# Rebuilding the joint stage of a fused two-layer block: plain fp32 products, scatter in 32-row pieces, new engine order

## The reference, cut to what matters

```
x = x + tanh(g_xattn[0]) * L0_xattn(layernorm(x), ctx, ctx, Wq..bo)   # 16 heads, strided mask
x = x + tanh(g_ffn[0])   * L0_ffn(layernorm(x), controller, f1, f2, bias)
x = x + tanh(g_xattn[1]) * L1_xattn(layernorm(x), ctx, ctx, mask)
x = x + tanh(g_ffn[1])   * L1_ffn(layernorm(x), ln_g, ln_b, w1, w2)

L0_ffn:  grouped = 16 tokens a group; logits = grouped @ controller; perm = (logits == max over the group)
         sel = perm^T @ grouped; inner = relu(sel @ f1 + bias); inter = inner @ f2      # 64 slots a group
         out[token] = sum over slots of perm[token, slot] * inter[group, slot]           # the scatter
L1_xattn: softmax(x @ ctx^T * 512**-0.5 + mask * -1e9) @ ctx                             # one head of width 512
L1_ffn:  h = layernorm(x) * ln_g + ln_b; int8 of h by a quantile of |h|; ternary w1; gelu; int8; ternary w2
```

## Time and profile before

| | |
|---|---|
| Median of 3 runs | 1605.69 us (1605.4 to 1609.05) |
| The profiled execution | 1610.68 us, of which the span of the trace is 1608.6 us |
| Joint stage in the trace | 821.9 to 1138.2 us |
| PE / PEld / DVE / ACT / POOL busy over the span | 81% / 58% / 64% / 47% / 27% |

### The profile page before, as it was taken

How to read it: one execution, slowest core, us unless ns; L and a number is a source line. 1 busy time by engine, 2 the same in 40 slices (tenths; PEclk the granted TensorE clock), 3 DMA queues, 4 the chain that set the end, 5 groups by cost and what they waited for, 6 DMA issues and landing times. The chain is left out here.

```text
span 1608.6 us, 25261 instructions
## 1 busy us (share of the span) xinstructions
PE 1304.2 (81%) x9084; PEld 935.0 (58%) x9106; DVE 1027.0 (64%) x2374; ACT 759.1 (47%) x1145; POOL 433.5 (27%) x435
## 2 busy tenths in 40 slices
PE   6999999999999559999958999995142799244996
PEld 5788888888888347666425666664132444142442
DVE  5677667767776434444325787877396488776774
ACT  3233343434333214564323555553473555486991
POOL 1233333333333201110014878775100000000021
PEclk9999999999999769999979999997555799655998
DMA  6122231223121196885699888841300277322974
GB/s 219 45 71 73 87 105 66 73 85 105 66 73 62 49 338 223 295 314 223 249 289 275 241 229 241 229 145 40 109 1 3 111 307 305 142 79 69 419 298 157
DMA packets 100471, 261.81 MB, mean 163 GB/s; under 512 B 11120, under 2 KB 22544, under 8 KB 93200
## 3 DMA queue, kind: packets, MB, share of 16 engines
q1 hardware_dynamic: 88704, 226.82, 40.6%
q0 software_dynamic: 8688, 32.51, 6.2%
q10 hardware_dynamic: 2976, 1.14, 0.3%
HBM read 155.32 MB, written 105.12 MB: 162 GB/s over the span
## 5 line engine op out<-in xcount | busy, mean ns | idle before, releaser
L1203 PE MATMUL p_s<-p_rows,p_permT 128*128 128x512 f32 x256 | 132.2, 614 | 6.1 <-DMA p_rows<-inter_d 4.0
L922 PEld LDWEIGHTS p_sel<-p_pick,p_xp 128*128 128x128 bf16 x1536 | 91.4, 101 | 57.2 <-issue 32.6
L922 PE MATMUL p_sel<-p_pick,p_xp 128*128 128x128 bf16 x1536 | 102.5, 226 | 23.8 <-DVE p_pick L1044 12.5
L2267 POOL DMA_DIRECT2D p_y<-residual x8 | 10.8, 1347 | 404.8 <-POOLq L113 343.2
L1934 PE MATMUL p_z<-qT,w1T 128*128 128x512 bf16 x501 | 112.6, 385 | 3.0 <-PEq L113 2.5
L1060 DVE COPY p_selT<-p_sel 128x512 f32<-128x512 f32 x64 | 44.3, 692 | 104.6 <-PE p_sel L922 104.6
L2291 PE MATMUL p_o<-w2T,p_Gq 128*128 128x512 bf16 x376 | 85.2, 384 | 8.8 <-DVE p_Gq L2348 8.5
L1993 DVE MAX8 cand<-hid 128x8 f32<-128x128 f32 x384 | 74.7, 277 | 25.2 <-ACT hid L1981 25.2
L1934 PEld LDWEIGHTS p_z<-qT,w1T 128*128 128x128 bf16 x512 | 50.6, 99 | 64.7 <-issue 5.9
L1005 ACT ACTIVATE p_selT<-p_sel 128x512 f32<-128x512 f32 x64 | 38.2, 597 | 91.4 <-PE p_sel L922 91.4
L342 PE MATMUL p_M<-p_ctxTh,p_Wkh 128*128 128x256 f32 x256 | 76.0, 297 | 1.9 <-DVE p_Wkl L668 1.9
(11 more groups left out here) (335 smaller groups left out, 3910.2 us busy)
## 6 DMA issues: line engine op xcount, KB each, us to landing
inter_d<-p_stage SPq DMA_DIRECT2D x64, 512.0 KB, 4.0
p_rows<-inter_d SPq DMA_DIRECT2D x128, 256.0 KB, 5.3
activations<-hid SPq DMA_DIRECT2D x24, 1024.0 KB, 3.9
p_cin<-in_ctx_dram SPq DMA_DIRECT2D x32, 512.0 KB, 5.3
xparts<-p_parts SPq DMA_DIRECT2D x16, 768.0 KB, 3.2
hid<-activations SPq DMA_DIRECT2D x10, 1024.0 KB, 9.6
p_xp<-xparts SPq DMA_DIRECT2D x3, 3072.0 KB, 25.3
p_xin<-in_x_dram SPq DMA_DIRECT2D x16, 512.0 KB, 4.3
```

The lines of the kernel that those rows point to most:

```text
L922: mm = pe.matmul(bsel[u % 2][:, k * P:(k + 1) * P], xp[:, c, tile, r, :], pick[sb % 2][:, tile, :, :].rearrange("p s g -> p (s g)"), start ...
L1203: mm = pe.matmul(bo[t][:, :], permT[b % 2][:, t, k, :], R[b % 2][:, t, k, :], start=(k == 0), stop=(k == NK - 1))
```

## The change

It touches the joint stage, the DRAM layout of the two residuals, and the loads of the residual in the last stage. The scatter becomes four matmuls a tile, each writing 32 rows (two groups) of the output from 128 rows of `inter_d` (2 groups by 64 slots), with weights of 32 columns; the rows of a tile come in one DMA with partition g*64+s. `spread` and `permT` shrink to 2 groups, so a batch needs 2 turns. Scores and attention are single fp32 matmuls on unsplit data: no `turned_lows`, `e_low`, `values_high`, `values_low`; the values are `cin` itself. x is only centred before it is turned (`nm`), and the factor rstd*512**-0.5 (`rs`) is applied in `logits`. Keys are taken in the order (p t), so that a partition's part of ctx is one piece of 4 KB; the mask is permuted to match. Depths grow (XD 6, CD 5, two buffers of e, mx, z, rz), turned exponentials get the bank `bE`, which the turned perm shares, and STEPS is 21.

```diff
-    XD, CD = 4, 3
+    XD, CD, AHEAD = 6, 5, 2
-        spread = [sbt(f"spread{i}", [P, NT, SL, GR], BF16) for i in range(2)]
-        permT = [sbt(f"permT{i}", [P, NT, NK, P]) for i in range(2)]
+        spread = [sbt(f"spread{i}", [P, NT, GH, SL], BF16) for i in range(2)]    # GH = 2
+        permT = [sbt(f"permT{i}", [P, NT, P]) for i in range(2)]
-        rows = inter_d.rearrange("(n g) (k s) d -> n k s g d", g=GR, s=SK)
+        ct = ctx.rearrange("b (p t) d -> b p t d", t=NT)
+        rows = inter_d.rearrange("(n h g) s d -> n (g s) h d", h=GR // GH, g=GH)
-        STEPS = B + 4
+        STEPS = B + 5
@@ SP
             def load_rows(b, t):
-                for k in range(NK):
-                    sp.dma_start(R[b % 2][:, t, k, :], rows[b * NT + t, k])...
+                if b >= 2:
+                    sp.wait_ge(s[f"scattered{t}"], b - 1)
+                sp.dma_start(R[b % 2][:, t, :, :], rows[b * NT + t])...
             for i in range(STEPS):
+                if live(i + 1):
+                    load_rows(i + 1, 1)
+                    load_x(i + 1)          # waits hh_done of i-5, x_out of i-5
+                    load_ctx(i + 1)        # waits O_full of i-4
+                if live(i + 2):
+                    load_rows(i + 2, 0)
+                if live(i + 1):
+                    load_mask(i + 1)
+                if live(i - 4):
+                    store(i - 4)
@@ PE
+            def scatter(b, t):
+                pe.wait_ge(s["permT_done"], b + 1)
+                pe.wait_ge(s[f"r_in{b % 2}{t}"], 16 * (b // 2 + 1))
+                if b >= 1:
+                    pe.wait_ge(s[f"added{t}"], b)
+                for h in range(GR // GH):
+                    toks = slice(h * TH, (h + 1) * TH)                          # TH = 32
+                    mm = pe.matmul(bo[t][toks, :], permT[b % 2][:, t, toks], R[b % 2][:, t, h, :], start=True, stop=True)
             def scores(b, t):
-                terms = [(c, a, w) for c in range(C) for a, w in ((0, 0), (0, 1), (1, 0))]
+                for c in range(C):
+                    mm = pe.matmul(bS[:, t * S:(t + 1) * S], xnT[:, c, t * P:(t + 1) * P], ctxT[b % 2][:, c, :], ...)
             def attend(b, t):
-                terms = [(k, a, w) for k in range(NT) for a, w in ((0, 0), (0, 1), (1, 0))]
+                for k in range(NT):
+                    mm = pe.matmul(bO[t][:, :], eT[:, k, t, :], cin[b % CD][:, k, :], ...)
+            for i in range(STEPS):
+                attend(i - 3, 0); turn_ctx(i - 1, 0); turn_perm(i); turn_ctx(i - 1, 1); attend(i - 3, 1)
+                turn_xn(i - 1, 0); scatter(i, 0); turn_xn(i - 1, 1); scores(i - 1, 0); scatter(i, 1)
+                turn_e(i - 2); scores(i - 1, 1)
@@ ACT, each step
+                hidden(i - 4, 0); hidden(i - 4, 1); ctx_out(i - 1, 0); ctx_out(i - 1, 1); centred(i - 1, 0)
+                permT_out(i); centred(i - 1, 1); xn_out(i - 1, 0); xn_out(i - 1, 1); exps(i - 2)
+                magnitudes(i - 4); e_turned(i - 2)
@@ POOL, each step
+                rstd1(i - 2); spreads(i + 2); gains(i - 4); rstd2(i - 3)
@@ DVE, each step
+                maxima(i - 5); variance1(i - 1); logits(i - 2); attended(i - 3, 0); softmax(i - 2)
+                attended(i - 3, 1); scale_mask(i - 1); add(i, 0); variance2(i - 3); inverse(i - 2); add(i, 1)
+            def logits(b):
+                for t in range(NT):
+                    dve.scalar_tensor_tensor(e[b % 2][:, t, :], bS[:, t * S:(t + 1) * S], rs[b % 2][:, t:t + 1],
+                                             mks[b % 2]..., ALU.mult, ALU.add).then_inc(s["S_taken"], 1)
@@ rstd1 on POOL takes 3 small operations as before, rstd2 takes 4 in place of 9
@@ ffn
-                    pool.dma_start(y[i % 2][:, :, :], xv[:, order[i] * WB:(order[i] + 1) * WB, :])...
+                    pool.dma_start(y[i % 2][:, :, :], x3_d[:, order[i] * WB:(order[i] + 1) * WB, :])...
@@ mk_flamingo_gated
-    x_one, x_three = [dram(f"residual{i}", (B, S, D)) for i in range(2)]
+    x_one, x_three = dram("residual0", (B, P, NT, D)), dram("residual1", (P, TILES, D))
```

More of the change, by code:

```diff
@@ L1115, in phase2b3 @@
         bo, bT, bO = [[ps(f"{n}{i}") for i in range(2)] for n in "sTO"]
[L1116 to L1119, removed]
+        bS, bE = ps("S"), ps("E")
+        halves = "scattered added norm cT_full c_out nT_full n_out S_full O_full x3_done hh_done".split()
+        names = """const_in ident_in ln_in identb_done mask2_done tanh_done spread_done turned permT_done mean1 rstd1 mask_done S_taken soft exp
+            e_full e_out rz_done var2 rstd2 hg_done hid_done abs_done max_done own own_pool""".split() + \
+            [f"{n}{t}" for n in halves for t in range(NT)] + \
             [f"x_in{i}" for i in range(XD)] + [f"x_out{i}" for i in range(XD)] + [f"c_in{i}" for i in range(CD)] + \
@@ L1193, in _ @@
         @block.tensor
         def _(pe):
[L1196 to L1205, removed]
@@ L1220, in turn_tile, with turn_ctx @@
                 mm.then_inc(full, 1)
-            def turn_ctx(b):
+            def turn_ctx(b, t):
                 pe.wait_ge(s[f"c_in{b % CD}"], 16 * (b // CD + 1))
[L1224 to L1233, removed]
@@ L1235, in scores @@
-            def scores(b, t):
[L1236 to L1240, removed]
-                terms = [(c, a, w) for c in range(C) for a, w in ((0, 0), (0, 1), (1, 0))]
[L1242 to L1245, removed]
+                if b >= 1:
+                    pe.wait_ge(s[f"n_out{t}"], b)
@@ new lines, in _ @@
+                if live(i - 3):
+                    attend(i - 3, 0)
+                if live(i - 1):
+                    turn_ctx(i - 1, 0)
+                if live(i):
+                    turn_perm(i)
+                if live(i - 1):
+                    turn_ctx(i - 1, 1)
+                if live(i - 3):
+                    attend(i - 3, 1)
+                if live(i - 1):
+                    turn_xn(i - 1, 0)
+                if live(i):
+                    scatter(i, 0)
+                if live(i - 1):
+                    turn_xn(i - 1, 1)
+                    scores(i - 1, 0)
@@ L1289, in _ @@
+                if live(i):
+                    scatter(i, 1)
+                if live(i - 2):
+                    turn_e(i - 2)
+                if live(i - 1):
+                    scores(i - 1, 1)
         @block.scalar
@@ L1315, in hidden @@
-            def hidden(b):
+                    wait_all(act, "O_full", b)
+                act.activation(eT[:, :, :, :], bE[:, :].rearrange("p (k t q) -> p k t q", k=NT, t=NT), ACT.Copy).then_inc(s["e_out"], 1)
+            def hidden(b, t):
                 act.wait_ge(s["rstd2"], b + 1)
@@ L1378, in _, with after @@
             of_all = lambda a: a[:, :].rearrange("p (a d) -> p a d", a=1).broadcast_to([P, NT, D])
-            def small(out, a, c, op, sem=None):
-                pool.tensor_tensor(out[:, :], a, c, op).then_inc(sem or own, 1)
-                if sem is None:
-                    pool.wait_ge(own, n.next(own))
+            def after(op):
+                op.then_inc(own, 1)
+                pool.wait_ge(own, n.next(own))
             def spreads(b):
@@ L1418, in values_low @@
[L1418 to L1420 removed]
+                if b >= 2:
+                    wait_all(pool, "hh_done", b - 1)
+                after(pool.tensor_scalar(w5[:, :], mv2[b % 2][:, :, 1], 1.0 + EPS, EPS * EPS, ALU.mult, ALU.add))
+                after(pool.tensor_tensor(w6[b % 2][:, :], w5[:, :], mhalf[:, :], ALU.pow))
@@ L1492, in maxima, with softmax @@
+            def softmax(b):
+                dve.wait_ge(s["S_taken"], NT * (b + 1))
+                dve.tensor_reduce(mx[b % 2][:, :], e[b % 2][:, :, :], AX.X, ALU.max).then_inc(own, 1)
+                dve.wait_ge(own, n.next(own))
+                dve.tensor_scalar(mx[b % 2][:, :], mx[b % 2][:, :], -1.0, None, ALU.mult).then_inc(s["soft"], 1)
             def maxima(b):
```

380 lines of the change are left out of this document (160 added, 220 removed).

## The result

The changed kernel takes 1514.58 us in the median (1511.18 to 1516.68, 4 runs), the kernel before 1607.37 (1605.4 to 1609.73, 4 runs): ratio 0.9413 with an interval of 0.9399 to 0.9427. The prediction was 1514.0. The profiled execution took 1514.46, its span is 1512.7.

A forecast was written before the change was run, and what follows sets the result against it. PE was taken to bound the joint stage. Fill to 863, 12 steps of 12.0 us to 1007 and a 38.5 us drain end it at 1045.5; 91.3 and 0.4 us less bring the median from 1605.7 to 1514.0, range 1502 to 1549.

The forecast's parts named there:

- PE's sum: Joint stage, steady step: PE's scatter, mode switches, scores, attention and turns add up to 11.5 us.
- Handshakes: Joint stage, steady step: handshakes among PE at 11.5, DMA at 10.8 and DVE at 10.7 make the step 12.0 us.
- second rival: Joint stage: handshakes make each step 12.9 us, 80 us less in all, time 1525; chance 0.15.
- Fill: Start of the joint stage: DMA brings 12.8 MB at 355 GB/s, batch 3's last scatter ends at about 863.
- Drain: End of the joint stage: from the last scatter of batch 15 to the stage's end, 38.5 us.
- Rows: Joint stage DMA: the new row order gives 345 to 360 GB/s, 10.6 to 11.0 us a batch.
- 4 KB pieces: Larger pieces for x_mid and ctx: part of the faster joint-stage DMA; outside the stage, for x_mid, no gain.
- DVE: Joint stage, steady step: DVE's busy time falls from 13.01 to 10.0 us, 10.7 with gaps, and does not bind.
- What bounds the kernel before: Joint stage of the kernel before: PE bounds, busy 15.42 of 16.34 us a step, with DMA not far behind.
- Rivals 3 and 4: Joint stage: scatter pieces do not run together, 1586, chance 0.05; PE's clock stays at its lower level, 1679, chance 0.02.
- fourth rival: Joint stage: PE's shorter work with more waits keeps its clock at 1.2 GHz, step 22.5 us, time 1679; chance 0.02.

The follow-up runs named there:

- full-width kernel: The changed kernel, but each of a batch's eight scatter matmuls writes all 128 rows, four accumulating in a bank; 1588.9 us, ratio 0.9878.

## Why the prediction was right, point by point

**PE's sum: right.** 11.5 foretold, 11.49 measured. The scatter with its switches took 2.29 instead of 2.26 a step (from the full-width kernel), the scores 3.46 instead of 3.44, attention 3.44. One reading was wrong without effect: 951.88 - 951.01 is the eight turns (0.87), the scatter matmul is 951.01 - 950.15 = 0.86.

**Handshakes: wrong.** "Three near-equal loads with handshakes cost something, and I take 12.0 us a step." They cost nothing in most steps; between 870 and 1000 PE waits once, 0.8 us. From batch 3 to batch 15 that is 138.9 instead of 144, 5.1 us. The second rival goes with it.

**Fill: wrong by about as much, the other way.** From the stage's first load to the end of batch 3's last scatter it is 45.9 us, where 863 - 821.9 = 41.1 was foretold. The bytes were there: by the windows the 12.8 MB had come at 859.1, 40.4 us behind the stage's first load. But from batch 2 (its last scatter at 852.1) to batch 3 (863.6) it is 11.5 us, PE's step. After batch 2 the fill was PE's and no longer DMA's, which my sum of bytes could not show: I priced the fill by DMA alone.

**Drain: right.** 39.3 instead of 38.5 us. In all the stage took 224.1 us up to the last maxima, 223.6 foretold. The errors of +4.8, -5.1 and +0.8 cancel, and that is luck. The profiled execution came to 1514.5 where 1519.0 was foretold: 3.2 by the earlier start, 1.5 behind the stage (1.9 where 0.4 was foretold), 0.3 outside the span, less 0.5. The median agrees to 0.6 us by luck again: I took 5.0 off as the distance of the profiled execution from the median, and that of after lies on its median, so this error of 5 hides the one of 4.5.

**Rows: right.** Old rows would have cost 28 us; 354 to 375 GB/s in place of 355 assumed. **4 KB pieces**: hidden, as the DMA share of 0.96 beside a full PE allows.

**DVE: wrong, without effect.** 10.0 busy foretold, 11.3 measured. The mask scaling, held by POOL, takes 1.99 instead of 0.28 us; the rest is 0.4 less than my sum.

**What bounds the kernel before: wrong, by a little.** "PE bounds the stage" stands on 94% busy, and my sum of 16.2 for PE counts its wait of 0.93. PE's own work was 15.4, and the ring shown above, 16.34, set the step. By the prediction's logic the new scatter alone, 5 us of PE's work less a step, should have given most of the gain. It cost 20 us. In the new order it is worth 74. The sum for the whole change came out right because I had followed the new order engine by engine, and the new order has no ring as long as PE's 11.5 us: `nm` no longer passes through POOL, five subtractions are gone, and `rs` is needed a step later. Which of these opens the ring is not settled: the new scatter with plain fp32 in the old order was not run. That PE is 99% busy in the old order without the splits says that there the ring is no longer than 16.8 us, no more.

**Rivals 3 and 4.** The pieces run together: eight records in 1.07 us, against 3.60 at full width. The clock was 1.00 in every steady step. The scatter-alone kernel shows that the fourth rival's mechanism is real: with PE busy 143.88 of 210 us and waits up to 6.6 us long, the grant over that stretch is 0.80, and the result is slower than before. How much of the 20 us is the clock's and how much the hold of `rz` is not separated.

## What to carry to other kernels

An engine at 94% busy may still not be what sets the step; here its one short wait in every step was the sign. Before cutting its work, follow the in-order queues around one step, and look for a ring of waits that does not pass through the work to be cut. Here there was one, and the cut gave idle time, and with it a lower clock. And read a short instruction's minimum beside its mean. `nm`, with a mean of 1.36 us and a minimum of 0.17, was held by another engine, and its place in the order decided whether that cost anything.

## What the runs showed of the hardware

- DVE's scaling instructions with input and output in SBUF are held while one of POOL's 128x1024 instructions runs, at both sizes seen: 128x2 in 2.18 us, or 2.41 against 0.23 in after; 128x256 in 1.99 against 0.28. The timelines of one step of after:

```profile
952.95 2.36 POOL L1402 TENSOR_TENSOR hid<-p_hh,p_lnb 128x1024 f32<-128x1024 f32 x1
...
953.47 1.99 DVE L1455 TENSOR_SCALAR p_masks<-p_mask 128x256 f32<-128x256 f32 x1
```

  Both end near 955.3 to 955.5. The Trainium skill (SBUF — State Buffer, SBUF: two separate sides) says that a VectorE operation in a mode with two ports and a GpSimd operation share one pair of ports, which the first takes for its whole instruction while the other is blocked. The trace agrees in that the held instruction ends with POOL's, and halving POOL's instruction halved the longest hold; which mode DVE ran in, no trace shows. Who came first is not always to be read off either: the 2.41 us one is recorded 0.03 us ahead of POOL's.
- Four 32-column pieces of 512 fp32 columns take 1.00 us up to the start of the next instruction, and 1.14 with all that switching costs its neighbours (2.29 for two), against 3.43 at full width (944.97 - 941.54 in the full-width kernel).
- Taking work from PE made two kernels slower (1514.6 to 1521.2, 1608.3 to 1628.5); in both PE then waited, up to 3.2 and 6.6 us at a time, and the granted clock fell, to 0.92 and 0.80 in the steps.
